# Two-layer kernel on one core: out products placed in a row ahead of the third row tile's convolution, in the middle units of the first layer

## The reference, cut to what matters

```python
q = conv4(h @ Wq); k = conv4(h @ Wk); v = conv4(h @ Wv)   # causal, depthwise, 4 taps
...                                                       # a rotating scan over the tokens gives out
o = out * rsqrt(mean(out**2) + eps) * rms_w * silu(h @ Wg)
x = x + o @ Wo                                            # out product and residual
h2 = layernorm(x)                                         # the second norm
aff = sigmoid(h2 @ centroids.T)                           # router: 16 experts, top 2
x = x + 0.1 * shared_swiglu(h2) + routed(h2)
```

## Time and profile before

| | |
|---|---|
| median of 3 runs | 2369.8 us (2368.15 to 2373.53) |
| the profiled execution: its own time, its span | 2383.38 us, 2381.6 us |
| granted TensorE clock, mean | 0.973 |
| busy share of PE, DVE, ACT, POOL | 93%, 81%, 56%, 23% |
| calls 1 to 3 in the profile | 95.5 to 423.8 us |

### The profile page before, as it was taken

How to read it: one execution, slowest core, us unless ns; L and a number is a source line. 1 busy time by engine, 2 the same in 40 slices (tenths; PEclk the granted TensorE clock), 3 DMA queues, 4 the chain that set the end, 5 groups by cost and what they waited for, 6 DMA issues and landing times. The chain is left out here.

```text
span 2381.6 us, 37757 instructions
## 1 busy us (share of the span) xinstructions
PE 2220.0 (93%) x13400; PEld 1927.5 (81%) x13400; DVE 1926.3 (81%) x4233; ACT 1341.4 (56%) x3105; POOL 545.4 (23%) x516
## 2 busy tenths in 40 slices
PE   6899999879999999999999999999999999999996
PEld 4677776757778888889889888888988888898894
DVE  6888887868877989887987988798798888879763
ACT  3544433015636656775675677567567656756752
POOL 0212232420114223212211312222132132122210
PEclk9899999888999999999999999999999999999998
DMA  8001000416531112112111211211121121111100
GB/s 275 1 1 49 23 32 23 169 45 206 170 102 58 36 54 76 41 36 64 61 36 36 89 36 40 73 48 41 53 67 45 41 72 54 36 50 49 40 1 18
DMA packets 88537, 145.95 MB, mean 61 GB/s; under 512 B 8352, under 2 KB 55840, under 8 KB 88352
## 3 DMA queue, kind: packets, MB, share of 16 engines
q1 hardware_dynamic: 67104, 112.07, 14.6%
q0 software_dynamic: 6144, 16.79, 2.0%
q10 hardware_dynamic: 15104, 14.68, 1.8%
HBM read 105.76 MB, written 37.75 MB: 60 GB/s over the span
## 5 line engine op out<-in xcount | busy, mean ns | idle before, releaser
L871 ACT ACTIVATE pr<-bank,negmax 128x128 f32<-128x128 f32 (+3 forms) x512 | 265.9, 526 | 274.7 <-DVE negmax L1365 220.9
L562 POOL TENSOR_TENSOR wo_low<-wraw_o,wo_high 128x256 fp32r<-128x256 f32 x128 | 95.2, 744 | 921.0 <-ACT wo_high L607 921.0
L1365 DVE TENSOR_REDUCE negmax<-bank 128x1 f32<-128x128 f32 (+3 forms) x512 | 239.6, 489 | 13.1
L552 POOL TENSOR_TENSOR wqk_low<-wraw,wqk_high 128x512 fp32r<-128x512 f32 x128 | 165.1, 1290 | 335.8 <-ACT wqk_high L607 335.8
L977 DVE TENSOR_TENSOR p_low<-bank,p_high 128x512 fp32r<-128x512 f32 (+1 forms) x384 | 206.8, 593 | 9.1 <-ACT p_high L607 0.6
L1391 DVE SCALAR_TENSOR_TENSOR xs<-bank,rinv,xs 128x256 f32<-128x256 f32 x512 | 211.2, 475 | 1.2 <-PE bank L1506 1.2
L1504 PE MATMUL bank<-h_high,wqk_high 128*128 128x512 f32 x512 | 203.4, 397 | 2.2 <-DVE h_low L977 2.2
L1505 PE MATMUL bank<-h_low,wqk_high 128*128 128x512 f32 x512 | 203.4, 397 | 0.0
L1506 PE MATMUL bank<-h_high,wqk_low 128*128 128x512 f32 x512 | 203.3, 397 | 0.0
L1504 PE MATMUL bank<-wo_high,z_high 128*128 128x256 f32 x512 | 149.4, 292 | 52.9 <-issue 35.4
L607 ACT ACTIVATE p_high<-bank 128x512 fp32r<-128x512 f32 (+1 forms) x384 | 173.0, 529 | 0.7 <-PE bank L1808 0.7
(11 more groups left out here) (284 smaller groups left out, 6593.5 us busy)
## 6 DMA issues: line engine op xcount, KB each, us to landing
wraw<-in_wpair SPq DMA_DIRECT2D x64, 512.0 KB
wraw<-in_wpair SPq DMA_DIRECT2D x64, 256.0 KB
wraw_o<-in_wpair SPq DMA_DIRECT2D x64, 256.0 KB, 2.6
tokens_by_expert<-zero SPq DMA_DIRECT2D x10, 1024.0 KB, 10.4
xt<-tokens_by_expert SPq DMA_DIRECT2D x40, 256.0 KB, 3.2
expert_results<-ey ACTq DMA_DIRECT2D x40, 256.0 KB, 3.6
wres<-in_wexp SPq DMA_DIRECT2D x1, 6144.0 KB, 19.6
xs<-x_between_stages SPq DMA_DIRECT2D x8, 512.0 KB
```

The lines of the kernel that those rows point to most:

```text
L552: pool.tensor_tensor(low, wraw[r][:, 2 * e * D:2 * (e + 1) * D], high.bitcast(F32), ALU.subtract).then_inc(s_wq, 1)
L562: pool.tensor_tensor(wo2[e][1][:], wraw_o[r][:, e, :], wo2[e][0][:].bitcast(F32), ALU.subtract).then_inc(s_wo, 1)
L871: ins = sc.activation(pr[:, i, 0:(i + 1) * P], score(i), ACT.Exp, bias=negmax[:, i:i + 1], accum_out=rsum[:, i:i + 1])
L1365: ins = v.tensor_reduce(negmax[:, i:i + 1], score(i), AX_X, ALU.max, negate=True)
```

## The change

PE: the two halves of the out product are issued one after the other, all four products of the third row tile come behind them, and the fill transposes behind that fall from 44 to 20. DVE: both residuals, both statistics and the second norm's chain come ahead of `conv_angle(y, 2)`. ACT: `router_norm` moves from behind `tap_value(y, 2)` to ahead of it, and `whole_turns(y, 2)` goes from ahead of `tap_value(y, 2)` to behind it.

```diff
-MIDDLE_TURNS = (12, 44)
+MIDDLE_TURNS = (12, 20)
...
                 tap_angle(y, 2)
+                router_norm(x)
+                tap_value(y, 2)
                 whole_turns(y, 2)
-                tap_value(y, 2)
-                router_norm(x)
                 router_input(x)
                 sin_cos(y, 2)
...
                 reduce_angle(y, 1)
-                residual(x, 0)
-                unit_stats(1, xu[x % 3], 0)
+                for ab in range(2):
+                    residual(x, ab)
+                    unit_stats(1, xu[x % 3], ab)
+                unit_norm(1, s_ln2)
                 conv_angle(y, 2)
-                residual(x, 1)
-                unit_stats(1, xu[x % 3], 1)
-                unit_norm(1, s_ln2)
                 conv_value(y, 2)
                 reduce_angle(y, 2)
...
                 conv_products(y, 1, (0, 1, 2, 3))
-                out_product(x, 0)
-                conv_products(y, 2, (0, 1))
-                out_product(x, 1)
-                conv_products(y, 2, (2, 3))
+                for ab in range(2):
+                    out_product(x, ab)
+                conv_products(y, 2, (0, 1, 2, 3))
                 pe.wait_ge(s_res, 2 * x + 1)
                 clock_turns(MIDDLE_TURNS[1], 6)
                 router_turn(x)
```

## The result

The kernel after took 2376.86 us (median of 20 runs, 2373.36 to 2379.81), the kernel before in the same comparison 2371.89 us (20 runs, 2366.62 to 2376.34): ratio 1.0023, 95% interval 1.0016 to 1.0030, so +5.5 us with 3.8 to 7.1. The change made the kernel slower, clear of zero. Whether it is beyond the 0.2% (4.7 us) that the prediction took for a difference is not settled: the interval reaches to both sides of it.

A forecast was written before the change was run, and what follows sets the result against it. DVE's chain was taken to bound call 1, with PE level, and PE to be later in calls 2 and 3. Terms +2.6, +1.4 and -0.2 gave +3.8 us on 2369.8: 2373.6 us, range 2367.0 to 2378.0.

The forecast's parts named there:

- The second out product 2.86 us earlier, ACT holding `hm`, logits 0.25 us earlier: Norm starts 2.86 us earlier, but whole_turns waits for DVE's convolution and holds the router's input: logits gain only 0.25 us.
- DVE 2.6 us late: DVE idles 4.5 us instead of 1.89 before the second residual; everything after conv_value(y, 2) comes 2.6 us later.
- The pause brings the clock down ahead of the logits in every call: PE stands still 3.4 us before the logits, the clock falls, and logits take 6.71 us in each call.
- The longer logits are hidden by DVE in calls 1 and 2: At the router's ranks DVE is later than PE in calls 1 and 2, so the slower logits add nothing there.
- The sum: Call 1 +2.6, call 2 +1.4 (1.23 was a wait for PE), call 3 -0.2: together +3.8 us.
- upper bound: Calls 1 and 2 pay 2.6 each, call 1's late PE another 0.3, call 3 +0.7: sum 6.2 us.
- The total: Whole kernel: 2369.8 + 3.8 = 2373.6 us, range 2367.0 to 2378.0.
- slower rival: DVE and PE both late, all three calls pay: 6.2 us, 2376.0 us; chance 0.33.
- lower bound: If call 1's PE were as late as call 2's, call 1 pays only 1.4 us: sum 2.4 us.
- PE's early end: Early end of the span in which PE reaches call 1's ranks, 182.7 to 183.9; DVE brings picks at 183.7.
- faster rival: PE's router chain sets the end; clock falls in pause and logits, shared products run at 2.4 GHz: -5.2 us, 2364.6; chance 0.12.
- What I took as covered by DVE: Cutting 24 fill transposes before the second norm's transposes moves the sum by nothing, since DVE is later.

The follow-up runs named there:

- the three kernels in which only PE or ACT was cured: Kernel after with 44 fill transposes, with 26 transposes in PE's pause, or with router_input ahead of whole_turns: ratios 1.0013, 1.0020, 1.0015 against the kernel before.
- `hm` ahead of turns: Kernel after with ACT's router_input moved ahead of whole_turns(y, 2): ratio 1.0015 (1.0006 to 1.0025) against the kernel before.
- the first experiment: Kernel before with only the fill cut, 20 transposes in place of 44: ratio 1.0022 (1.0012 to 1.0032), +5.2 us.
- the one that took 10 us more: Kernel after with ACT's router_input directly behind router_norm, ahead of tap_value and whole_turns: ratio 1.0043 (1.0029 to 1.0057) against before, 5 runs.

## Why the prediction was right, and what it mis-sized

- **The second out product 2.86 us earlier, ACT holding `hm`, logits 0.25 us earlier**: held. The second residual comes 7.37 us behind the first where it came 10.12, 2.75 earlier, the logits only 0.12 earlier.
- **DVE 2.6 us late**: held. The wait was 4.64 us against 4.5 forecast; from the first residual to `bia` went from 29.43 to 32.16 us, 2.7 more. That this alone lengthens calls 1 and 2 is shown by the three kernels in which only PE or ACT was cured: all stayed at 39.83 to 39.86.
- **The pause brings the clock down ahead of the logits in every call**: held, at 3.4 to 3.5 us, and the logits took 7.01 rather than 6.71. The length of the pause alone does not decide it: behind 44 transposes a pause of 2.35 us left the logits at 5.14, behind 20 one of 1.98 us (`hm` ahead of turns) brought them to 6.70. The Trainium skill, TensorE: Matmul & The Clock Gate, section Why this matters for your kernels, warns of pauses between bursts; the trace agrees, with 0.70 in the three microseconds that hold most of the pause.
- **The longer logits are hidden by DVE in calls 1 and 2**: held, but barely. In call 3, which PE sets alone, the ranks come at 38.35 us and `places` at 39.23, against 38.40 and 39.86 in call 1: PE was 0.05 us from setting the ranks and 0.6 from setting `places`.
- **The sum**: call 1 +2.6 forecast, +2.73 in the profiles; call 2 +1.4, +1.40; call 3 -0.2, +0.82. The mis-sized term is call 3. I let PE start its logits 0.25 us earlier and keep 6.71 and 9.12 us; it started 0.19 us earlier counted from the first residual, and took 7.01 and 9.82. The lower clock ruled the whole of the logits and more of the shared products. Only the upper bound had held room for that (+0.7). Against the 36.79 us that the same call took in another execution, its term would be +2.4, so the sizes for calls 2 and 3 hold only for the trace of before that I read.
- **The total**: the 2376.86 us lie in the range of 2367.0 to 2378.0, 3.3 above the 2373.6 forecast. Of these, 2.1 are the kernel before, whose median was 2369.8 in 3 runs and 2371.89 in 20. Of the change, +3.8 us was forecast and +5.5 (3.8 to 7.1) measured. That is in the slower rival's band, beyond 4.7, and nearer to its 6.2, though the interval takes in both.
- **The slower rival** is half of what happened. Its condition, both engines late and all three calls paying, is what the experiments show; its price for call 2 is not, since that call paid 1.40 and not 2.6 in the profiles. Its chance of 0.33 was not too high.
- **Slips in the working**: the lower bound should read 1.4 + 1.4 - 0.2 = 2.6, not 2.4, and PE's early end 167.25 + 6.55 + 9.0 = 182.8, not 182.7. Neither moves the forecast.
- **The faster rival** fell: it needed shared products of 7.11 us, but they began at the lower clock (0.50 from 173 to 176 us) and took 9.77 to 9.82 us (9.06 to 10.08 before). Besides, PE is not alone on the path of calls 1 and 2. Whether the early norm pays where DVE's lateness is gone is not clearly shown: the lowest ratio there, 0.9982 (0.9973 to 0.9991), and that of the kernel before with the statistics moved, 0.9991 (0.9982 to 1.0001), overlap.
- **What I took as covered by DVE**, cutting 24 transposes, is the other full cause. I did not say what it would cost uncovered: +5.2 us (2.8 to 7.6) by the first experiment.

## What to carry to other kernels

When a trace shows two engines level at a meeting point, price each one's lateness separately and write down the larger; a cure for one will measure as nothing until the other is cured too, and that is no proof that it was the wrong cure. When work is pulled ahead, look through the consumer's own queue for an instruction that waits for the very work that was pushed back: here `whole_turns` and the router's input. And look at what filled the wait that the new order opens: the next unit's norm fits DVE's waits of 2.1 and 4.6 us, and fill belongs in the stretch where PE now pauses.

## What the runs showed of the hardware

Transposes of the identity, here in fp32, hold TensorE's clock up. In the same pause of 3.46 us, 26 of them brought the logits from 7.01 to 5.37 us; the granted clock from 163 to 166 us was 1.00 with them, where it was 0.70 from 164 to 167 without. The Trainium skill, TensorE: Matmul & The Clock Gate, Part 4: PE-mode transpose, says that transposes don't count as work for the clock; here the measurement decides against it. They also lift it: in the kernel before, 40 of them ran alone from 443.15 us for 5.98 us, and the clock was 0.50 from 443 to 446 us, 0.97 in the next microsecond and 1.00 in the two behind it.

Where the clock falls changes the time of one execution outside the changed code too. In the front of call 3 the kernel before ran two stretches at 0.84 and 0.82 that the kernel after ran at 1.00. The windows of before, then of after:

```profile
330.00:335.00 5.00, 4.58 (x31) 4.07 (x30) 4.93 (x7) 1.78 (x4) 0.10 (x1) 0.84 0.00 0
335.00:340.00 5.00, 5.00 (x28) 4.34 (x27) 4.79 (x7) 3.24 (x6) 4.41 (x4) 0.82 0.06 26
```

```profile
330.00:335.00 5.00, 4.64 (x28) 3.83 (x28) 4.96 (x5) 2.23 (x4) 2.73 (x2) 1.00 0.00 0
335.00:340.00 5.00, 4.94 (x32) 4.43 (x32) 4.89 (x7) 1.73 (x5) 1.73 (x2) 1.00 0.00 0
```

From call 2's `shared_down` to call 3's first residual that was 65.89 us against 63.43, 2.5 us in a stretch that the change doesn't touch. The same kind of dip, 64.97 to 65.1 us against 63.4 to 63.6, shows in one of two such stretches of five other kernels, among them the one that took 10 us more. I did not settle what brings it on; it is of the size of the effects measured here. Behind call 3's `places`, in code that all thirteen kernels share, their profiles take from 1963.5 to 1974.1 us, before the longest. Together these are why one profiled execution can point the wrong way.
